# A language tower on one Trainium2 core: the first group's output projection, norm and turn are placed earlier in the banded attention loop

## The chip, the cores and the metric

The kernel is one program on one core of a Trainium2 chip. The metric is device time in microseconds (us) of one execution. Before the change three runs gave 1850.09, 1851.66 and 1854.64 us, with the median 1851.66 us. The engines are named as in the profile: PE is the matrix engine (PEld its weight loads), DVE the vector engine, ACT the scalar engine, POOL the GpSimd engine, SP the queue that issues the DMAs.

## The reference, cut to what matters

2048 tokens (8 sequences of 256) with 192 features pass four layers of banded attention with 12 heads of 16 features and a hidden layer of 768. After them come a cross-covariance attention, an expert layer with 4 experts, a full attention and an expert layer with 8 experts, which the change does not touch.

```python
h = layer_norm(emb_word[input_ids] + emb_pos[:S][None], emb_ln_s, emb_ln_b)
for l in range(L):                                     # L = 4
    q, k, v = heads(h @ Wq[l] + bq[l]), heads(h @ Wk[l] + bk[l]), heads(h @ Wv[l] + bv[l])
    a = band_attention(q, k, v, mask)                  # each query sees keys within 64 positions
    a = a.transpose(0, 2, 1, 3).reshape(B, S, Hd)
    h = layer_norm(h + a @ Wo[l] + bo[l], ln1_s[l], ln1_b[l])
    f = jax.nn.gelu(h @ W1[l] + b1[l], approximate=False)
    h = layer_norm(h + f @ W2[l] + b2[l], ln2_s[l], ln2_b[l])
```

## The kernel before, in words

Every engine has its own program, written out in order, and waits for the others on counting semaphores. The order in which work stands is therefore fixed by the code. The tokens lie in 16 tiles of 128 (`NT`), in 4 groups (`NG`) of 4 tiles (`GT`). A tile of `h` or of the attention's result `xn` must have its features on the partitions before a projection can read it. So it is turned: PE transposes it in two halves (line 417), ACT copies it into `xx` (line 638), DVE takes what the rounding left (lines 751 and 752). `xn` is turned for the output projection (kind 1 in `turned`, called "att" in the loop), `h` for the hidden layer (kind 2).

The attention loop of a layer (`pe_attention`, `act_attention`, `dve_attention`) has 96 iterations p, each for one head of one sequence. PE computes scores (lines 528 and 530), DVE their negated maximum (778), ACT the exponentials (671), PE turns the probabilities (549), ACT and DVE split them in a high part (684) and a low part (785), and PE multiplies with the values (570 to 572). After every sixth iteration DVE sums and inverts the denominators (803, 808 and 811, here the "finish"), and POOL scales the result into `xn` (1028). The loop of DVE goes on after its last maximum, until the last values are finished; this is called the drain below.

At even iterations a side step stands in the loop. `STEPS` places the projections of later groups ("chunk", "v") and the turns of `h` that feed them ("tile"). `LATE` places, in iterations 70 to 92, four turns of `xn` (tiles 0 to 3), four output projections of these tiles ("out", PE lines 445 to 449 and DVE line 741, which adds the residual into `h`), and four more turns of `xn` (tiles 4 to 7). All of these side steps share one PSUM bank, so a step waits until the one before it has been read. DVE takes statistics of group 0 at iteration 88 (884 and 888), POOL computes the inverse deviation (972 and 973), and DVE normalises the four tiles in iterations 94 to 101 (`dve_norm_step`: line 834 at even steps, 840 and 843 at odd ones).

After the loop PE projects the output of tiles 4 to 7 (`pe_out_group`; DVE adds at 875), turns `h` of group 0 (`pe_turn(pe, it, 2, 0, 8)`), and then begins the hidden layer. `pe_hidden` has steps n = 0 to 25: a step computes one block of 128 hidden features for a group of 512 tokens (five matmuls, lines 435 to 439, a "hidden block" below), ACT applies the Gelu (720), and two steps later PE multiplies with the second weight (631, 16 matmuls). `under` places turns and output projections of later groups between these steps: group 1 of `h` before step 2, group 2 of `xn` before step 3, the output of group 2 before step 5, and so on. `dve_tail` and `pool_tail` follow this order; the norm after the loop is lines 918 to 927. The first projections of the next layer stand between the last hidden blocks.

Of the kernel before, what the change touches and what calls it, by code (L numbers as in the profile page):

```python
# [34 lines left out]
NG, GT = 4, 4  # L35
# [19 lines left out]
LATE = (70, 72, 74, 76, 78, 80, 82, 84, 86, 88, 90, 92)  # L55
TURNED = ((1, 0), (1, 1), (2, 0), (2, 1), (1, 2), (2, 2), (1, 3), (2, 3))
# [49 lines left out]
def build_tower(nc, a, out, stop=None):  # L106
    ctx = ExitStack()
    with ctx:
# [256 lines left out]
        def step(p, banded):  # L365

            g, k = p // PAIRS_G + 1, p % PAIRS_G
            if banded and p in LATE:
                i = LATE.index(p)
                return ("att", "out")[i // GT % 2], i % GT + GT * (i // (2 * GT)), None  # L370
            if g < NG and k in STEPS:
                kind, i = STEPS[k]
                if kind != "tile":
                    return kind, g, i
                if g + 1 < NG:
                    return kind, GT * (g + 1) + i, None
            return None

        def pe_step(pe, it, p, banded, w, w_out, tile, xx):
# [4 lines left out]
            if back:  # L384
                kind, a, b = back[-1]
                if kind == "chunk":
                    pe.wait_ge(qf_ready.sem, qf_ready.at(it, 3 * a + b + 1))
                elif kind == "v":
                    pe.wait_ge(vf_ready.sem, vf_ready.at(it, 4 * a + b + 1))
                elif kind == "tile":  # L390
                    pe.wait_ge(xx_ready.sem, xx_ready.at(*xx(a + 1)))
                elif kind == "att":
                    pe.wait_ge(xx_ready.sem, xx_ready.at(it, turned(1, a) + 1))
                else:
                    pe.wait_ge(o_read.sem, o_read.at(it, a + 1))
# [5 lines left out]
            elif kind == "tile":  # L401
                tile(a, True)
            elif kind == "att":
                pe_transpose(pe, it, turned(1, a), a, xn, att_ready, it, a // 2 * 2 + 2, True)
            else:
                if a % GT == 0:
                    pe.wait_ge(wb_ready.sem, wb_ready.at(it, 1))
                    pe.wait_ge(xx_ready.sem, xx_ready.at(it, turned(1, a + GT - 1) + 1))
                pe_tokens(bank[BM[0]][:, 0:D], w_out, 0, D, a).then_inc(o_done.sem, 1)
# [94 lines left out]
        def under(turn, out=None, first=None):  # L504

            steps = {}
            for g in range(NG - 1):
                steps[FC * g + 2] = lambda g=g: turn(2, g + 1)
                if g + 2 < NG:
                    steps[FC * g + 3] = lambda g=g: turn(1, g + 2)  # L510
# [94 lines left out]
        def pe_out_group(pe, it, w, g):  # L605

            for t in range(GT * g, GT * g + GT):
                pe.wait_ge(xx_ready.sem, xx_ready.at(it, turned(1, t) + (3 if t % GT < 2 else 1)))
# [4 lines left out]
        def pe_hidden(pe, it, w, w2, sigs, before):  # L613

            u_done, f_ready, y_done, y_read = sigs
            for n in range(NG * FC + 2):
# [8 lines left out]
                if n >= 2:  # L625
                    g, c = (n - 2) // FC, (n - 2) % FC
                    pe.wait_ge(f_ready.sem, f_ready.at(it, n - 1))
                    for t in range(GT):
# [64 lines left out]
        def act_attention(act, it, banded, tile):  # L693

            for p in range(PAIRS + 3):
# [6 lines left out]
                if step(p, banded):  # L702
# [5 lines left out]
                    elif kind == "att":  # L708
                        act_split(act, it, turned(1, a), a, True)

# [17 lines left out]
        def dve_step(dve, ch, it, p, banded, tile):  # L728

            if p and step(p - 1, banded):  # L730
# [5 lines left out]
                elif kind == "att":  # L736
                    dve_split(dve, it, turned(1, a), a, True)
                elif kind == "out":
# [4 lines left out]
            if banded and p == LATE[2 * GT - 1] + 4:  # L743
                dve_stats(dve, ch, it, 0, 0, o_read)
            if banded:
                dve_norm_step(dve, ch, it, p - LATE[2 * GT - 1] - 10, NORMED.index((1, 0)) + 1, 0, 0)

# [183 lines left out]
        def dve_tail(dve, ch, it, opening):  # L931
# [9 lines left out]
            dve_turn(dve, it, 2, 0)  # L941
            for g in range(NG + 1):
# [8 lines left out]
                if g + 2 < NG:  # L951
# [759 lines left out]
        def _(pool):  # L1711
# [27 lines left out]
            def pool_layer(it, opening):  # L1739
# [21 lines left out]
                for f in range(NT - 5, NT):  # L1761
                    if f == NT - 3:
# [62 lines left out]
        def _(act):  # L1825
# [6 lines left out]
            def act_layer(it, opening):  # L1832
                act_attention(act, it, True, first_split(it))
                act_turn(act, it, 2, 0)
# [186 lines left out]
        def _(pe):  # L2021
# [14 lines left out]
            def pe_layer(it, opening):  # L2036
                pe_attention(pe, it, True, wa, first_turn(it), lambda n: (it, n), wb)
                pe_out_group(pe, it, wb, 1)
                pe_turn(pe, it, 2, 0, 8)
                pe_hidden(pe, it, wb, w2[0], tok_hidden,  # L2040
                          under(lambda k, g: pe_turn(pe, it, k, g, 12 if (k, g) == (2, 2) else
                                                     16 if (k, g) == (2, 3) else None),
# [181 lines left out]
```

## Time and profile before

| | us |
|---|---|
| median of the three runs | 1851.66 |
| the profiled execution's own time | 1853.58 |
| its span, first to last instruction | 1851.5 |
| PE busy in the span | 1469.3 (79%) |
| DVE busy | 1243.0 (67%) |
| ACT busy | 979.6 (53%) |
| POOL busy | 818.5 (44%) |

The profiled execution took 1853.58 us, 2.1 us more than its span, and lies inside the range of the three runs. Its mean granted PE clock is 0.899. A busy share is a mean over stages with different limits: in the attention loop DVE is nearly always busy, in the hidden layer PE is. The rows of the windows below are of layer 0, the last of the first group of layer 3. In a row of the timeline the number in brackets is how long the engine was idle before that row, and what ended the idleness. A row's start minus the start of the row before is what the instruction costs in a busy queue, since the ends overlap with the next start.

### The profile page before, as it was taken

What the parts mean: (1) busy time and instruction counts of PE and PEld (TensorE: products, weight loads), DVE (VectorE), ACT (ScalarE), POOL (GpSimd) and SP (SyncE); (2) the same over time, 40 slices, a digit from 0 to 9 for tenths busy, and PEclk for the clock granted to TensorE, in tenths of its full rate; (3) what the DMA queues carried; (4) which work ended last, traced back from release to release, by engine and by line L of the source; (5) the groups of instructions that cost most, each with busy time, mean ns of one, the idle gap of its engine ahead of it and who ended that gap; (6) DMA issues with size and microseconds to landing.
All of it is one profiled execution on the core that took longest, in us unless ns stands there. A gap on an engine that the chain in (4) does not pass through costs nothing.

```text
span 1851.5 us, 39522 instructions
## 1 busy us (share of the span) xinstructions
PE 1469.3 (79%) x13098; PEld 1230.7 (66%) x13098; DVE 1243.0 (67%) x3542; ACT 979.6 (53%) x2391; POOL 818.5 (44%) x1177
## 2 busy tenths in 40 slices
PE   0589889888898987998879769759658887599991
PEld 0467678677686776777767648539646666489991
DVE  4788966889668887768886642434388897434444
ACT  0478633788335885358863123235348882155550
POOL 5577233774236852357623410125456421145540
PEclk9999999999899998999989857679869996589996
DMA  4666101743007440054600000147534411268765
GB/s 120 172 152 124 31 1 39 164 96 77 1 5 177 99 93 1 1 133 96 143 3 1 9 6 1 35 147 237 163 87 104 106 35 35 80 203 244 236 208 178
DMA packets 144278, 177.87 MB, mean 96 GB/s; under 512 B 22096, under 2 KB 106128, under 8 KB 143952
## 3 DMA queue, kind: packets, MB, share of 16 engines
q1 hardware_dynamic: 136784, 158.18, 33.5%
q0 software_dynamic: 7296, 17.18, 2.8%
q8 instruction: 108, 1.77, 0.4%
q14 instruction: 90, 0.74, 0.1%
HBM read 132.96 MB, written 42.34 MB: 95 GB/s over the span
## 4 chain that ended last, share of the span: by engine, by line
PE 53%; DVE 26%; issue 9%; POOL 4%; DMA 4%; ACT 2%; SPq 2%; DVEq 0%; POOLq 0%; ACTq 0%
DVE ptl L785 7%; PE bank L1459 7%; PE bank L631 7%; PE bank L549 3%; DVE neg_max L778 3%; PE bank L417 2%; PE bank L570 2%; PE bank L435 2%; PE bank L437 2%; PE bank L436 2%; PE bank L1445 2%; PE bank L438 2%; PE bank L439 2%; PE bank L530 2%; DVE xx L752 2%
## 5 line engine op out<-in xcount | busy, mean ns | idle before, releaser
L671 ACT ACTIVATE prob<-bank,neg_max 128x192 f32<-128x192 f32 (+1 forms) x960 | 407.3, 437 | 115.8 <-DVE neg_max L778 102.1
L778 DVE TENSOR_REDUCE neg_max<-bank 128x2 f32<-128x384 f32 (+1 forms) x480 | 274.4, 573 | 85.9 <-PE bank L530 85.0
L785 DVE TENSOR_TENSOR ptl<-bank,pth 128x384 f16<-128x384 f32 (+1 forms) x480 | 276.1, 575 | 4.9 <-ACT pth L684 4.1
L549 PE MATMUL bank<-ident,prob 128*128 128x128 f32 x1536 | 268.5, 288 | 0.0
L684 ACT ACTIVATE pth<-bank 128x384 f16<-128x384 f32 (+1 forms) x480 | 244.5, 509 | 9.1 <-PE bank L549 8.9
L638 ACT ACTIVATE xx<-bank 128x256 fp32r<-128x256 f32 x256 | 95.6, 386 | 196.4 <-PE bank L417 192.4
L530 PE MATMUL bank<-kx,qx 96*128 96x192 bf16 (+1 forms) x960 | 166.3, 255 | 1.1 <-DVE xx L752 1.1
L549 PEld LDWEIGHTS bank<-ident,prob 128*128 128x128 f32 x1536 | 163.0, 143 | 0.0
L570 PE MATMUL bank<-v,pth 128*128 128x33 bf16 x1152 | 138.3, 180 | 20.7 <-DVE ptl L785 17.8
L720 ACT ACTIVATE fbuf<-bank,b 128x512 f32<-128x512 f32 x96 | 65.9, 687 | 155.3 <-PE bank L439 155.3
L631 PE MATMUL bank<-w,fbuf 128*128 128x192 f32 x768 | 140.7, 327 | 2.0 <-DVE h L875 2.0
L972 POOL TENSOR_SCALAR rstd<-mv 128x4 f32<-128x4 f32 x52 | 13.3, 255 | 287.1 <-DVE mv L888 280.9
L631 PEld LDWEIGHTS bank<-w,fbuf 128*128 128x128 f32 x768 | 128.5, 190 | 12.2 <-issue 5.2
L572 PE MATMUL bank<-v,ptl 128*128 128x33 bf16 x1152 | 136.4, 178 | 0.0
L571 PE MATMUL bank<-v,pth 128*128 128x16 bf16 x1152 | 132.6, 170 | 0.0
L528 PE MATMUL bank<-mask,ident 128*128 128x384 bf16 x384 | 128.5, 335 | 2.7 <-DVE xx L752 1.1
L1382 POOL DMA_INDIRECT y_rows<-vf,mask x68 | 78.9, 1160 | 117.0 <-DVE vf L1536 101.3
L570 PEld LDWEIGHTS bank<-v,pth 128*128 128x128 f16 x1152 | 99.4, 96 | 42.8 <-DVE ptl L785 42.2
L530 PEld LDWEIGHTS bank<-kx,qx 96*128 96x128 bf16 x960 | 94.3, 100 | 34.6 <-issue 3.1
L417 PE MATMUL bank<-ident,h 128*128 128x128 f32 x256 | 52.4, 310 | 81.4 <-DVE h L927 46.4
L1459 PE MATMUL bank<-w,fbuf 128*128 128x192 f32 x552 | 112.1, 327 | 0.0
L417 PE MATMUL bank<-ident,xn 128*128 128x128 f32 x256 | 57.0, 338 | 66.1 <-DVE xn L898 32.4
(295 smaller groups left out, 4519.2 us busy)
## 6 DMA issues: line engine op xcount, KB each, us to landing
xn<-in_e_seg SPq DMA_DIRECT2D x34, 768.0 KB, 6.6
w<-in_e_w SPq DMA_DIRECT2D x23, 576.0 KB, 4.1
qk_rows<-fbuf SPq DMA_DIRECT2D x128, 96.0 KB, 2.3
qx<-qk_rows SPq DMA_DIRECT2D x35, 288.0 KB, 4.0
kx<-qk_rows SPq DMA_DIRECT2D x35, 288.0 KB, 5.8
qk_rows<-w SPq DMA_DIRECT2D x80, 96.0 KB, 2.3
qx<-qk_rows SPq DMA_DIRECT2D x35, 192.0 KB, 4.6
kx<-qk_rows SPq DMA_DIRECT2D x35, 192.0 KB, 5.4
```

The source lines that it names most:

```text
L417: last = nc.tensor.transpose(o[:, c * P:c * P + P], src[:, t, c * P:c * P + P], ident[:, :])
L530: last = nc.tensor.matmul(o[:, qt, :], qx[0:ROWS, b % 3, hd, qt * P:qt * P + P], kx[0:ROWS, b % 3, hd, keys(qt, banded)], start=not banded ...
L549: last = nc.tensor.transpose(bank[BT[p % 2]][:, c * P:c * P + P], probs_at(p, banded, c * P, P), ident[:, :])
L570: nc.tensor.matmul(o, pth[:, p % 3, w], v[sums], start=first, stop=False)
L571: nc.tensor.matmul(o[third], pth[:, p % 3, w], v[lows], start=False, stop=False)
L572: return nc.tensor.matmul(o, ptl[:, p % 2, w], v[sums], start=False, stop=stop)
L631: last = nc.tensor.matmul(bank[BY[t]][:, 0:D], fbuf[:, (n - 2) % 4, t * P:t * P + P], w2[:, c, :], start=(c == 0), stop=(c == FC - 1))
L671: nc.scalar.activation(probs_at(p, banded, qt * n, n), scores_at(p, n)[:, qt, :], ACT.Exp, bias=neg_max[:, b % 2, hd, qt:qt + 1], scale=1. ...
L684: nc.scalar.activation(pth[:, p % 3, 0:n], bank[BT[p % 2]][:, 0:n], ACT.Copy).then_inc(hi_ready.sem, 1)
L778: nc.vector.tensor_reduce(neg_max[:, b % 2, hd, :], scores_at(p, D if banded else S), AX.X, ALU.max, negate=True).then_inc(max_ready.sem, 1)
L785: nc.vector.tensor_tensor(ptl[:, p % 2, 0:n], bank[BT[p % 2]][:, 0:n], pth[:, p % 3, 0:n], ALU.subtract)\
L1459: last = nc.tensor.matmul(bank[BY[2 * (G % 2) + s]][:, 0:D], fbuf[:, n % 4, s * P:s * P + P], w2_e[G % 3][:, c, :], start=(c == 0), stop=( ...
```

## The change: what it does

The side steps in the loop are laid out anew. The four turns of `xn` of group 0 move from iterations 70 to 76 to 52, 54, 58 and 60, where the last group of queries has no "tile" steps. The four output projections move from 78 to 84 to 70 to 76, the turns of `xn` of tiles 4 to 7 from 86 to 92 to 78 to 84. The statistics of group 0 move from iteration 88 to 80, its norm steps from 94 to 101 to 86 to 93. The turn of the normed `h` of group 0, which stood after the loop, becomes four side steps of kind "h" at iterations 88 to 94, on PE, ACT and DVE. POOL computes the inverse deviation one scaling step earlier. Nothing is computed anew and nothing is left out.

After the loop the hidden layer now follows the output projections of tiles 4 to 7 directly. The turn of group 2 of `xn` moves from step 3 to step 1 of the hidden layer, that of group 1 of `h` from step 2 to step 4. At step 2 PE gets one more wait, for the last finish, since the second product writes banks that the attention has used.

```diff
--- before.py
+++ after.py
@@ -54,4 +54,6 @@
          14: ("v", 0), 16: ("v", 1), 18: ("v", 2), 20: ("v", 3)}
-LATE = (70, 72, 74, 76, 78, 80, 82, 84, 86, 88, 90, 92)
-TURNED = ((1, 0), (1, 1), (2, 0), (2, 1), (1, 2), (2, 2), (1, 3), (2, 3))
+LATE = {52: ("att", 0), 54: ("att", 1), 58: ("att", 2), 60: ("att", 3), 70: ("out", 0), 72: ("out", 1), 74: ("out", 2), 76: ("out", 3),
+        78: ("att", 4), 80: ("att", 5), 82: ("att", 6), 84: ("att", 7), 88: ("h", 0), 90: ("h", 1), 92: ("h", 2), 94: ("h", 3)}
+LATE_STATS, LATE_NORM = 80, 86
+TURNED = ((1, 0), (1, 1), (2, 0), (1, 2), (2, 1), (2, 2), (1, 3), (2, 3))
 LAST_TURNS = ((0, 0), (0, 1), (0, 2), (1, 0), (0, 3), (1, 1), (1, 2), (1, 3))
@@ -368,4 +370,3 @@
             if banded and p in LATE:
-                i = LATE.index(p)
-                return ("att", "out")[i // GT % 2], i % GT + GT * (i // (2 * GT)), None
+                return LATE[p] + (None,)
             if g < NG and k in STEPS:
@@ -393,2 +394,4 @@
                     pe.wait_ge(xx_ready.sem, xx_ready.at(it, turned(1, a) + 1))
+                elif kind == "h":
+                    pe.wait_ge(xx_ready.sem, xx_ready.at(it, turned(2, a) + 1))
                 else:
@@ -404,2 +407,4 @@
                 pe_transpose(pe, it, turned(1, a), a, xn, att_ready, it, a // 2 * 2 + 2, True)
+            elif kind == "h":
+                pe_transpose(pe, it, turned(2, a), a, h, h_ready, it, normed(1, a), True)
             else:
@@ -507,5 +512,5 @@
             for g in range(NG - 1):
-                steps[FC * g + 2] = lambda g=g: turn(2, g + 1)
+                steps[FC * g + (2 if g else 4)] = lambda g=g: turn(2, g + 1)
                 if g + 2 < NG:
-                    steps[FC * g + 3] = lambda g=g: turn(1, g + 2)
+                    steps[FC * g + (3 if g else 1)] = lambda g=g: turn(1, g + 2)
                     if out:
@@ -607,3 +612,7 @@
             for t in range(GT * g, GT * g + GT):
-                pe.wait_ge(xx_ready.sem, xx_ready.at(it, turned(1, t) + (3 if t % GT < 2 else 1)))
+                pe.wait_ge(xx_ready.sem, xx_ready.at(it, turned(1, t) + 1))
+                if g == 2 and t % GT < 2:
+                    pe.wait_ge(xx_ready.sem, xx_ready.at(it, turned(2, t - 2) + 1))
+                elif g == 3 and t % GT < 2:
+                    pe.wait_ge(xx_ready.sem, xx_ready.at(it, turned(1, t + 2) + 1))
                 if t % GT >= 2:
@@ -627,2 +636,4 @@
                     pe.wait_ge(f_ready.sem, f_ready.at(it, n - 1))
+                    if n == 2:
+                        pe.wait_ge(sums_ready.sem, sums_ready.at(it, NT))
                     for t in range(GT):
@@ -709,2 +720,4 @@
                         act_split(act, it, turned(1, a), a, True)
+                    elif kind == "h":
+                        act_split(act, it, turned(2, a), a, True)
 
@@ -737,2 +750,4 @@
                     dve_split(dve, it, turned(1, a), a, True)
+                elif kind == "h":
+                    dve_split(dve, it, turned(2, a), a, True)
                 elif kind == "out":
@@ -742,6 +757,6 @@
                         .then_inc(o_read.sem, 1)
-            if banded and p == LATE[2 * GT - 1] + 4:
+            if banded and p == LATE_STATS:
                 dve_stats(dve, ch, it, 0, 0, o_read)
             if banded:
-                dve_norm_step(dve, ch, it, p - LATE[2 * GT - 1] - 10, NORMED.index((1, 0)) + 1, 0, 0)
+                dve_norm_step(dve, ch, it, p - LATE_NORM, NORMED.index((1, 0)) + 1, 0, 0)
 
@@ -940,3 +955,3 @@
             out(1)
-            dve_turn(dve, it, 2, 0)
+            dve_turn(dve, it, 1, 2)
             for g in range(NG + 1):
@@ -950,3 +965,3 @@
                     dve_stats(dve, ch, it, 1, g - 1, y_read)
-                if g + 2 < NG:
+                if g and g + 2 < NG:
                     dve_turn(dve, it, 1, g + 2)
@@ -1761,3 +1776,3 @@
                 for f in range(NT - 5, NT):
-                    if f == NT - 3:
+                    if f == NT - 4:
                         pool_rstd(pool, ch, it, NORMED.index((1, 0)) + 1, 0, 1e-12)
@@ -1833,3 +1848,2 @@
                 act_attention(act, it, True, first_split(it))
-                act_turn(act, it, 2, 0)
                 act_hidden(act, it, b1[0], tok_hidden, ACT.Gelu,
@@ -2038,6 +2052,4 @@
                 pe_out_group(pe, it, wb, 1)
-                pe_turn(pe, it, 2, 0, 8)
                 pe_hidden(pe, it, wb, w2[0], tok_hidden,
-                          under(lambda k, g: pe_turn(pe, it, k, g, 12 if (k, g) == (2, 2) else
-                                                     16 if (k, g) == (2, 3) else None),
+                          under(lambda k, g: pe_turn(pe, it, k, g, {(1, 2): 8, (2, 2): 12, (2, 3): 16}.get((k, g))),
                                 lambda g: pe_out_group(pe, it, wb, g),
```

PE after the loop, layer 0, before the change. The first row is the last matmul of the output projection of tile 7; 435 to 439 are one hidden block each, 417 with `h` a turn of one group.

```order
L449 MATMUL bank<-wb_second_lo,xx 128x192
L417 MATMUL bank<-ident,h 128x128 x8
L435 MATMUL bank<-xx,wb_hi 128x512
...
L439 MATMUL bank<-xx,wb_second_lo 128x512
L417 MATMUL bank<-ident,h 128x128 x8
L435 MATMUL bank<-xx,wb_hi 128x512
...
L631 MATMUL bank<-w_0,fbuf 128x192 x4
L417 MATMUL bank<-ident,xn 128x128 x8
```

The same place after the change (the lines are those of the new file: 454 for 449, 422 for 417, 440 to 444 for 435 to 439, 642 for 631).

```order
L454 MATMUL bank<-wb_second_lo,xx 128x192
L440 MATMUL bank<-xx,wb_hi 128x512
...
L444 MATMUL bank<-xx,wb_second_lo 128x512
L422 MATMUL bank<-ident,xn 128x128 x8
L440 MATMUL bank<-xx,wb_hi 128x512
...
L642 MATMUL bank<-w_0,fbuf 128x192 x4
L422 MATMUL bank<-ident,h 128x128 x8
```

One turn, that of group 0 of `h`, is gone from here, and the first turn between the hidden blocks is that of `xn`. 

DVE in the drain, layer 0, before: from the low part of iteration 92 (785) to the residual of tiles 4 to 7 (875).

```order
L785 TENSOR_TENSOR ptl<-bank,pth 128x384
L840 SCALAR_TENSOR_TENSOR h<-hb,rstd,ln_b 128x128
L843 SCALAR_TENSOR_TENSOR h<-hb,rstd,ln_b 128x128
L785 TENSOR_TENSOR ptl<-bank,pth 128x384
L834 SCALAR_TENSOR_TENSOR hb<-h,mv,ln_s 128x192
...
L803 SCALAR_TENSOR_TENSOR rs<-stats,pad_keys,bank 128x6 x2
L808 TENSOR_REDUCE au<-bank 128x192
L811 RECIPROCAL rs<-rs 128x12
L875 TENSOR_TENSOR h<-bank,hb 128x192 x4
```

The same place after the change (800 for 785, 818 to 826 for 803 to 811, 890 for 875).

```order
L800 TENSOR_TENSOR ptl<-bank,pth 128x384
L826 RECIPROCAL rs<-rs 128x12
L800 TENSOR_TENSOR ptl<-bank,pth 128x384 x3
L818 SCALAR_TENSOR_TENSOR rs<-stats,pad_keys,bank 128x6 x2
L823 TENSOR_REDUCE au<-bank 128x192
L826 RECIPROCAL rs<-rs 128x12
L890 TENSOR_TENSOR h<-bank,hb 128x192 x4
```

The norm steps have left the drain. They now stand inside the loop; this is DVE of layer 0 after the change, from iteration 88 (849 and 855, 858 are the norm steps, 793 the maximum, 766 and 767 the split of a turned tile).

```order
L849 SCALAR_TENSOR_TENSOR hb<-h,mv,ln_s 128x192
L793 TENSOR_REDUCE neg_max<-bank 128x2
L800 TENSOR_TENSOR ptl<-bank,pth 128x384
L766 TENSOR_TENSOR xx<-bank,xx 128x128
L767 SCALAR_TENSOR_TENSOR xx<-xx,columns,bank 128x128
L855 SCALAR_TENSOR_TENSOR h<-hb,rstd,ln_b 128x128
L858 SCALAR_TENSOR_TENSOR h<-hb,rstd,ln_b 128x128
L818 SCALAR_TENSOR_TENSOR rs<-stats,pad_keys,bank 128x6 x2
L823 TENSOR_REDUCE au<-bank 128x192
```

## Rows read from the trace of the kernel before

**Rows 1.** Windows view: stretch, length, PE PEld DVE ACT POOL busy, clock, DMA; loop.

```profile
159.26:172.72 13.46, 11.73 (x160) 9.05 (x161) 11.42 (x30) 12.13 (x35) 9.20 (x13) 1.00 0.27 63
...
183.96:195.45 11.49, 10.35 (x145) 8.24 (x143) 11.27 (x33) 10.43 (x32) 6.40 (x13) 1.00 0.62 138
195.45:206.15 10.70, 9.63 (x131) 7.89 (x130) 9.60 (x27) 8.40 (x24) 4.27 (x6) 1.00 0.01 2
206.15:218.08 11.93, 9.70 (x138) 7.54 (x136) 11.73 (x37) 9.82 (x30) 2.16 (x4) 1.00 0.01 2
...
942.42:955.61 13.19, 10.97 (x138) 8.75 (x136) 11.77 (x37) 10.24 (x31) 2.16 (x4) 0.87 0.01 2
```

**Rows 2.** Windows view, loop's end to hidden step 5: layers 0, 1, all four.

```profile
225.21:250.63 25.42, 19.48 (x101) 15.67 (x96) 15.62 (x56) 8.99 (x18) 7.15 (x12) 0.80 0.00 1
469.87:495.68 25.81, 21.11 (x100) 17.10 (x96) 15.73 (x56) 8.99 (x18) 7.15 (x12) 0.74 0.00 1
...
sum 103.20, PE 82.39 PEld 66.33 DVE 62.77 ACT 35.96 POOL 28.57; mean PE 20.60 PEld 16.58 DVE 15.69 ACT 8.99 POOL 7.14
```

**Rows 3.** Windows view, the rest of the hidden layer, layer 0.

```profile
250.63:322.58 71.95, 67.01 (x380) 58.88 (x379) 49.09 (x173) 24.88 (x46) 26.89 (x41) 1.00 0.10 24
```

**Rows 4.** PE's timeline after the loop, layer 0: start, duration, engine, line.

```profile
225.21 0.34 PE L445 MATMUL bank<-wb_hi,xx 128*128 128x192 f32 x1
...
227.75 0.50 PE L445 MATMUL bank<-wb_hi,xx 128*128 128x192 f32 x1 [1.20 <-DVE h L875]
...
229.97 1.41 PE L417 MATMUL bank<-ident,h 128*128 128x128 f32 x4
...
234.76 0.80 PE L435 MATMUL bank<-xx,wb_hi 128*128 128x512 f32 x1 [1.06 <-DVE xx L752]
...
238.47 0.60 PE L417 MATMUL bank<-ident,h 128*128 128x128 f32 x4
...
241.05 0.48 PE L435 MATMUL bank<-xx,wb_hi 128*128 128x512 f32 x1
...
242.30 1.46 PE L631 MATMUL bank<-w,fbuf 128*128 128x192 f32 x8
243.60 0.60 PE L417 MATMUL bank<-ident,xn 128*128 128x128 f32 x4
...
245.74 0.48 PE L435 MATMUL bank<-xx,wb_hi 128*128 128x512 f32 x1
```

**Rows 5.** Windows view, the stretch of low clock at the loop's end, layer 1.

```profile
466.29:483.35 17.06, 13.98 (x80) 10.98 (x79) 13.78 (x47) 4.48 (x8) 6.40 (x11) 0.50 0.00 0
```

**Rows 6.** DVE's timeline, end of the loop and drain, layer 0.

```profile
209.69 1.13 DVE L884 BATCH_NORM_STATS2 stats<-h 128x6 f32<-128x192 f32 x4
...
211.07 0.53 DVE L778 TENSOR_REDUCE neg_max<-bank 128x2 f32<-128x384 f32 x1
...
217.62 0.29 DVE L751 TENSOR_TENSOR xx<-bank,xx 128x128 fp32r<-128x128 f32 x1
...
218.08 0.55 DVE L778 TENSOR_REDUCE neg_max<-bank 128x2 f32<-128x384 f32 x1
...
219.01 0.41 DVE L834 SCALAR_TENSOR_TENSOR hb<-h,mv,ln_s 128x192 f32<-128x192 f32 x1
219.34 0.56 DVE L778 TENSOR_REDUCE neg_max<-bank 128x2 f32<-128x384 f32 x1
...
220.27 0.35 DVE L840 SCALAR_TENSOR_TENSOR h<-hb,rstd,ln_b 128x128 f32<-128x128 f32 x1
...
220.79 0.35 DVE L803 SCALAR_TENSOR_TENSOR rs<-stats,pad_keys,bank 128x6 f32<-128x6 f32 x2
...
222.45 0.50 DVE L785 TENSOR_TENSOR ptl<-bank,pth 128x384 f16<-128x384 f32 x1
...
224.34 0.56 DVE L785 TENSOR_TENSOR ptl<-bank,pth 128x384 f16<-128x384 f32 x1
...
227.32 0.56 DVE L875 TENSOR_TENSOR h<-bank,hb 128x192 f32<-128x192 f32 x2
```

## The prediction

> **What bounds the kernel now.** I read the windows view of a layer first, then the timelines of PE and DVE where it showed a change of limit. In the loop DVE sets the pace: in iterations 70 to 78 of layer 0 it is busy 11.27 of 11.49 us, in 86 to 94 11.73 of 11.93 us, while PE has 10.35 and 9.70 us of work [rows 1]. The reader is to see that a window of eight iterations is as long as DVE's work in it plus about 0.2 us. The exception is a window with side steps heavy for PE: with four output projections (78 to 86) DVE works 9.60 of 10.70 us. In the hidden layer PE sets the pace, 67.01 of 71.95 us at full clock [rows 3], so what is won or lost before it shifts all that follows. Between the two lies the stretch from the first output projection after the loop (I call its start O, 225.21 in layer 0) to that of group 2. It takes 25.42 us in layer 0 and 103.20 us over the four layers, 25.80 each, of which PE is busy 20.60, at a mean granted clock of 0.80 in layer 0 [rows 2].
>
> PE's timeline shows what that stretch holds [rows 4]. PE waits 1.20 us for DVE's residual, then turns `h` of group 0: from 229.97 to 234.76, 4.79 us, for eight transposes that wait for ACT's copies and DVE's splits in turns. Everything from 227.75 to nearly 238.47 stands in a stretch at the lower of the clock's two levels, 1.2 instead of 2.4 GHz: a pair of output projections takes 2.22 us there (227.75 to 229.97) against 1.34 (225.21 to 226.55) before. In layer 1 the low clock spans 17.06 us and begins at 466.29, before O at 469.87 [rows 2, 5].
>
> **The change part by part: the loop.** The prices come from DVE's starts [rows 6]. An iteration without a side step costs 0.93 us (218.08 to 219.01), a split 0.46 (217.62 to 218.08), an even norm step 0.33 (219.01 to 219.34), an odd one 0.52 (220.27 to 220.79), the statistics 1.38 (209.69 to 211.07).
>
> Iterations 52 to 62 get four splits, 1.84 us of DVE, four ACT copies and eight transposes. DVE is idle there 13.46 - 11.42 = 2.04 us [rows 1], so the bounds are 0 and 1.84. Much of the idleness is one wait at the projection in iteration 56, where no split stands, and ACT has only 1.33 us left for its four copies. I take 1.4.
>
> Iterations 70 to 78 get the projections for the turns. That is the window 78 to 86 of before, 10.70 us, with most of a second finish in it, which I put at 0.4: 11.1 against 11.49, so -0.4 (bounds -0.8 and 0).
>
> Iterations 78 to 86 get four splits and the statistics, which is what 86 to 94 held: 11.93 against 10.70, +1.2.
>
> Iterations 86 to 94 lose one split and the statistics and get eight norm steps: 4 x (0.33 + 0.52) - 0.46 - 1.38 = +1.56. Iteration 94 loses a norm step, -0.33.
>
> The drain, from the last maximum (219.34) to O, took 5.87 us. Of DVE's norm steps 2.22 us leave it ahead of the last low part, and one split (0.46) comes in, so the bounds are -1.76 and 0. But the low part of one iteration lets PE turn the one two later, and ACT and DVE follow: 222.45 to 224.34 is 1.89 us for two iterations, DVE's own work in it barely more. With the norm steps gone this chain is late next, and I take -0.4.
>
> Sum of the loop: 1.4 - 0.4 + 1.2 + 1.56 - 0.33 - 0.4 = +3.0 us a layer. The new turns wait on PE for the norm of the tile, one iteration earlier on DVE. Behind them in PE's queue stand the next scores; DVE needs these only after its next maximum, so I price the wait at nothing, and if that cover is gone it costs up to 0.3 a step, 1.2 a layer. POOL's inverse deviation comes before a scaling that is not due yet. SP issues nothing new and is moved past nothing.
>
> **The stretch after O.** The finish starts with the last values, as the norm steps that stood before it are gone; PE's 1.20 us of waiting shrink to 0.3 (bounds 0 and 1.20). Then, at full clock: a pair of projections 1.25, the wait 0.3, the second pair 1.25, hidden block 0 1.25 (241.05 to 242.30), the turn of `xn` in step 1 at 2.58 (the price of 238.47 to 241.05, the same kind with a Gelu ahead of it), block 1 1.25, block 2 with its product 2.55 (241.05 to 243.60), the same for step 3, the turn of `h` in step 4 at 2.14 (243.60 to 245.74), and step 4 2.55 [rows 4]. Sum: 17.7 us. The turn in step 4 needs the norm of group 1, whose path over POOL starts with DVE's statistics as before, and it is due some 13 us after O; that norm lies under steps 1 to 3.
>
> The low clock is the unknown. It costs nothing if PE stays at full clock, and if it stays low for ten us of work 5. In layer 0 two blocks took 3.71 us (234.76 to 238.47) against 2.5 at full clock, so some 2.4 us of low clock came after the blocks had begun [rows 4]; now they begin within 3 to 5 us of O. I take five us of low clock, 2.5 lost: 20.2 us against 25.80, -5.6 a layer, bounds -8.1 and -3.1.
>
> One more term: PE has fewer matmuls per us in iterations 86 to 94, about 9.5 in 13.5 us against 9.70 in 11.93, and layer 3 shows what a low stretch costs there, 13.19 us at clock 0.87 against 11.93 at 1.00 [rows 1]. I take a third of it, +0.4.
>
> The page "TensorE: Matmul & The Clock Gate" of the Trainium skill (section "What's actually happening") says that the lower clock is the default state and that activity releases it. By it the gap-free blocks after O shorten the low stretch, but the thinner stretch before O may call it earlier. Which of the two is larger the rule does not tell; the rows price both, and the first would give rival B, the second rival D.
>
> **Sum.** +3.0 + 0.4 - 5.6 = -2.2 us a layer, -8.8 in four. The profiled execution took 1853.58 us, so 1844.8; it lies 1.9 above the median of the runs, and from the median, 1851.66, it is 1843.
>
> **The rivals.** B, the clock stays high: with PE busy from O on, no low stretch or a very short one. -8.1 + 3.0 = -5.1 a layer, 1831. For it speaks the missing gap of 4.79 us, against it that in layer 1 the low clock came 3.6 us before O.
>
> C, the stall is moved, not removed: the turn of `xn` in step 1 has no product beside it, and DVE comes to it only after four residuals and the statistics, ACT only after the first Gelu. If it costs what the turn after the loop did, 4.79 instead of 2.58, the layer gains nothing: 1852. Against it speaks that the statistics (1.38) fit under block 0.
>
> D, slower: the low clock begins with the norm steps. The place is iteration 86 to O, about 19 us. The price from layer 3: 1.26 us for 13 percent of 13.19, which at half rate is 3.4 us of low clock, so 0.37 us for each. Nineteen cost 7.0, the layer +4.4, the kernel 1869. It decides from 2.6 / 0.37 = 7 us of low clock before O in each layer. For it speaks that layer 3 dropped there once; against it that layer 0, with the same load, kept the full clock in its loop's end [rows 1].
>
> **How the numbers follow.** The forecast has 0.54, with its own range 1838 to 1848; B 0.18, C 0.17, D 0.11. A difference under 0.3%, 5.6 us, cannot be told from no change here. Faster by more: 0.48 of the forecast's and B, 0.66. Within: C and 0.05 of the forecast's, 0.22. Slower: D and the rest, 0.12. The range reaches to B and C and leaves most of D out: 1830 to 1854.
>
> **What would show it.** The window of iterations 86 to 94 should be 13.3 to 13.5 us, 78 to 86 11.9, 52 to 62 14.8, and the drain about 5.5. From O to the output of group 2 it should be 19 to 22 us, with block 0 right behind the fourth projection and the turn of `xn` at 2.6. The forecast is wrong if that stretch is over 23 us or the loop longer by over 4.5. The rest of the hidden layer should stay at about 72.

## The result and the profile after

The changed kernel took 1841.12 us (median of nine runs, 1835.38 to 1846.83), the kernel before beside it 1854.93 (nine runs, 1850.09 to 1862.84). The ratio is 0.9919, with a 95% interval of 0.9898 to 0.994. The forecast was 1843, a gain of 8.8 us; the gain between these medians is 13.8. Two later sets of six runs gave 0.993 (0.9914 to 0.9946) and 0.9916 (0.9886 to 0.9947).

The page of the profiled execution, which with 1835.38 us was the fastest of the nine, shows nearly the same work in a shorter span:

```profile
span 1833.3 us, 39538 instructions
PE 1455.2 (79%) x13098; PEld 1223.2 (67%) x13098; DVE 1242.2 (68%) x3542; ACT 979.3 (53%) x2391; POOL 815.4 (44%) x1177
```

The windows view answers to [rows 1] with the first four rows (iterations 52 to 62, 70 to 78, 78 to 86, 86 to 94 of layer 0), and then 86 to 94 of layer 1:

```profile
159.08:174.15 15.07, 12.81 (x173) 10.30 (x174) 13.22 (x38) 13.11 (x39) 9.45 (x13) 1.00 0.28 66
...
185.16:197.16 12.00, 11.20 (x155) 9.56 (x154) 10.33 (x28) 9.70 (x28) 6.46 (x13) 1.00 0.49 117
197.16:208.96 11.80, 9.07 (x127) 6.87 (x124) 11.76 (x39) 9.37 (x28) 5.48 (x8) 1.00 0.01 2
208.96:221.97 13.01, 10.29 (x130) 7.22 (x128) 13.01 (x39) 10.16 (x30) 0.89 (x2) 1.00 0.00 1
451.06:464.35 13.29, 11.16 (x130) 8.36 (x128) 13.11 (x39) 10.39 (x30) 0.88 (x2) 0.87 0.01 1
```

DVE is busy for 11.76 of 11.80 us in 78 to 86 and all the time in 86 to 94 (13.01 of 13.01). In 70 to 78 it has 1.67 us of idleness. The loop from iteration 52 to O took 69.57, 69.85, 69.49 and 69.48 us in the four layers, against 65.95, 66.59, 66.85 and 67.23 before: 2.94 us more a layer. In layer 0 of the kernel before, and in layers 2 and 3 of the changed one, the low clock does not occur between iteration 52 and O, and there the difference is larger, 69.49 less 65.95 or 3.5 us: before, low clock ahead of O had lengthened layers 1 to 3 (66.59 to 67.23). The drain was 5.73 us in layer 0 and 5.65 in layers 2 and 3.

The same view of the stretch from O to the output of group 2, of layers 0 to 3 and their sum, and of the rest of the hidden layer of layer 0 (against [rows 2, 3]):

```profile
228.65:248.33 19.68, 17.37 (x92) 15.14 (x88) 12.31 (x44) 6.51 (x14) 6.89 (x12) 0.84 0.00 1
471.05:490.72 19.67, 17.36 (x92) 15.11 (x88) 12.31 (x44) 6.50 (x14) 6.87 (x12) 0.84 0.00 1
714.40:733.24 18.84, 16.25 (x93) 13.93 (x88) 12.27 (x44) 6.59 (x14) 6.87 (x12) 0.91 0.00 1
956.78:975.62 18.84, 16.24 (x92) 13.92 (x88) 12.33 (x44) 6.59 (x14) 6.88 (x12) 0.91 0.00 1
...
sum 77.03, PE 67.21 PEld 58.10 DVE 49.22 ACT 26.19 POOL 27.52; mean PE 16.80 PEld 14.53 DVE 12.30 ACT 6.55 POOL 6.88
...
248.33:320.45 72.12, 67.16 (x381) 58.98 (x380) 50.10 (x173) 25.07 (x46) 25.96 (x41) 1.00 0.10 24
```

77.03 against 103.20 is 6.54 us less a layer, and the rest did not move. So the layer gains 3.6 us from iteration 52 on, four layers 14.4; some 1.2 of it are lost again in iterations 0 to 52 and ahead of them, since at the output of group 2 of layer 3 the changed kernel is 13.2 us ahead (975.62 against 988.85). The spans differ by 18.2. The other 5.0 us lie in later stages that the change does not touch, and they are within the scatter of one program: from that point to the end the kernel before took 862.6 us, and three profiles of the changed kernel 857.7, 869.5 and 865.3 (this one, c0 and c1 below).

PE's timeline after the loop, to be read against [rows 4]:

```profile
228.65 0.51 PE L450 MATMUL bank<-wb_hi,xx 128*128 128x192 f32 x1
...
232.80 0.41 PE L454 MATMUL bank<-wb_second_lo,xx 128*128 128x192 f32 x1
233.01 0.68 PE L440 MATMUL bank<-xx,wb_hi 128*128 128x512 f32 x1
...
235.07 0.60 PE L422 MATMUL bank<-ident,xn 128*128 128x128 f32 x4
236.96 0.87 PE L422 MATMUL bank<-ident,xn 128*128 128x128 f32 x4 [1.29 <-DVE xx L767]
237.58 0.48 PE L440 MATMUL bank<-xx,wb_hi 128*128 128x512 f32 x1
...
243.77 0.60 PE L422 MATMUL bank<-ident,h 128*128 128x128 f32 x4
245.29 0.87 PE L422 MATMUL bank<-ident,h 128*128 128x128 f32 x4 [0.93 <-DVE xx L767]
245.92 0.48 PE L440 MATMUL bank<-xx,wb_hi 128*128 128x512 f32 x1
```

The hidden block at 233.01 stands right behind the last projection. The turn of `xn` takes 2.51 us (235.07 to 237.58), that of `h` 2.15 (243.77 to 245.92). In both PE waits, 1.29 and 0.93 us, for ACT's copy and DVE's split of the first tiles.

### The profile page after: what moved, and what is told of

It reads as the page before. It is cut to its first block, busy times and chain, and to the rows that moved or that the text cites. A ratio compares the mean times of both kernels' runs of the same rounds, so it can differ in the third digit from the quotient of the medians.

```text
span 1833.3 us, 39538 instructions
## 1 busy us (share of the span) xinstructions
PE 1455.2 (79%) x13098; PEld 1223.2 (67%) x13098; DVE 1242.2 (68%) x3542; ACT 979.3 (53%) x2391; POOL 815.4 (44%) x1177
## 3 DMA queue, kind: packets, MB, share of 16 engines
q8 instruction: 108, 1.77, 0.4%
## 4 chain that ended last, share of the span: by engine, by line
PE 50%; DVE 25%; issue 9%; POOL 6%; DMA 4%; ACT 3%; SPq 2%; DVEq 0%; POOLq 0%; ACTq 0%
PE bank L1474 7%; PE bank L642 7%; DVE ptl L800 7%; DVE neg_max L793 3%; PE bank L554 3%; PE bank L422 2%; PE bank L1460 2%; PE bank L440 2%; PE bank L441 2%; PE bank L442 2%; PE bank L575 2%; PE bank L443 2%; PE bank L444 2%; DVE xn L913 2%; DVE xx L767 1%
## 5 line engine op out<-in xcount | busy, mean ns | idle before, releaser
L987 POOL TENSOR_SCALAR rstd<-mv 128x4 f32<-128x4 f32 x52 | 13.2, 255 | 245.1 <-DVE mv L903 239.1
L1043 POOL TENSOR_TENSOR xn<-au,rs 128x192 f32<-128x192 f32 x80 | 41.4, 518 | 157.5 <-DVE rs L826 155.2
```

## The experiments

Each kernel is timed against the kernel before on the same chip. "The stretch" below is O to the output of group 2.

**c0_after**, the change itself, as the base of the first set.

> The changed kernel itself, as the one against which the other kernels of this call are read. By all theories it is 12 to 16 us faster than the kernel before, as its nine runs were; from the loop's end to the output of group 2 it takes 19 to 20 us a layer.

1842.49 us, 0.993 (0.9914 to 0.9946). Its stretches were 19.70, 19.82, 17.26 and 17.25 us. The windows of layers 0 and 2, and of what follows in layer 2 up to the next loop:

```profile
228.91:248.61 19.70, 17.39 (x91) 15.15 (x88) 11.28 (x44) 6.50 (x14) 7.98 (x12) 0.84 0.00 1
714.12:731.38 17.26, 14.66 (x93) 12.49 (x88) 12.73 (x44) 6.57 (x14) 7.00 (x12) 1.00 0.00 1
731.38:805.92 74.54, 69.36 (x394) 60.41 (x392) 52.61 (x185) 25.37 (x46) 27.88 (x44) 1.00 0.11 28
```

The stretch at full clock is 17.25 us, with 0.29 us of waiting between the two pairs of output projections (at 715.75); the same program paid 2.45 us more in a layer with 6.3 us of low clock (a mean clock of 0.84 over 19.70 us, the lower level being half of the full one), and 1.59 more with 3.4 us (18.84 above). The next profile, **c1_after**, had 18.84, 19.75, 19.48 and 18.84: which layers see the lower clock differs between executions.

> The changed kernel itself once more, for the two others of this call: 12 to 16 us faster than the kernel before by all theories.

1839.64 us, 0.9916 (0.9886 to 0.9947).

**e1_loop_only**: the new layout of the loop, with `h` still turned after it and the hidden order of before. The diff is against the change and shows only the two lines that matter.

```diff
-        78: ("att", 4), ..., 84: ("att", 7), 88: ("h", 0), 90: ("h", 1), 92: ("h", 2), 94: ("h", 3)}
+        78: ("att", 4), ..., 84: ("att", 7)}
 ...
                 pe_out_group(pe, it, wb, 1)
+                pe_turn(pe, it, 2, 0, 8)
```

> The kernel before with only the loop laid out anew: output projection, statistics and norm of group 0 early as in the change, but its normed tiles are still turned after the loop, and the hidden layer's order is that of before. Theory 1 (the gain comes from the turn of 4.8 us that left the stretch after the loop): iterations 52 to 95 get 2.4 us a layer longer, the drain loses 0.4, PE's wait of 1.2 us loses 0.9, so the kernel is 2 to 6 us slower than before. Rival (the gain comes from the norm that left the drain and from the clock): it keeps most of the gain, 8 to 14 us faster than before.

1853.79 us, 0.9991 (0.9977 to 1.0005): no difference that can be told, where a small loss was expected. The windows of the stretch in layers 0 and 2, and of the drain in layer 0:

```profile
227.44:251.54 24.10, 19.04 (x100) 15.07 (x96) 14.76 (x52) 8.99 (x18) 7.15 (x12) 0.86 0.00 1
717.09:740.45 23.36, 18.09 (x101) 14.50 (x96) 14.80 (x52) 8.99 (x18) 7.08 (x12) 0.93 0.00 1
222.18:227.44 5.26, 3.76 (x66) 2.73 (x67) 4.04 (x11) 3.38 (x10) 0.52 (x1) 1.00 0.02 3
```

The earlier projection and norm cost the loop 1.9 us a layer up to its last maximum. The drain (5.26 or 5.27 us in the four layers, 6.17 in the mean before) gave 0.9 back and the stretch, with its shorter low clock, 2.1 (23.7 in the mean against 25.80). So the gain does not come from the earlier projection and norm by themselves.

**e2_old_hidden_order**: the change, but with the turns between the hidden blocks as before (`h` of group 1 before step 2, `xn` of group 2 before step 3).

```diff
-                steps[FC * g + (2 if g else 4)] = lambda g=g: turn(2, g + 1)
+                steps[FC * g + 2] = lambda g=g: turn(2, g + 1)
-                    steps[FC * g + (3 if g else 1)] = lambda g=g: turn(1, g + 2)
+                    steps[FC * g + 3] = lambda g=g: turn(1, g + 2)
```

> The changed kernel with the hidden layer's order of before: h of group 1 is turned before step 2 and xn of group 2 before step 3. Theory 1 (the two turns had to change places, since the norm of group 1 now ends too late for step 2): PE waits 3.5 to 6 us for the norm before step 2, so the kernel is 14 to 22 us slower than the changed one, about as fast as before. Rival (the order is indifferent, the turn costs the same wherever it stands): within 4 us of the changed one.

1867.05 us, 1.0063 (1.0045 to 1.0082): 25 us slower than the change, where 14 to 22 were expected. The timeline of PE in layer 0, with DVE's last norm instruction of tile 4 (L940), and the window of the stretch in layer 2:

```profile
233.62 0.39 PE L444 MATMUL bank<-xx,wb_second_lo 128*128 128x512 f32 x1
238.09 0.34 DVE L940 SCALAR_TENSOR_TENSOR h<-hb,rstd,ln_b 128x128 f32<-128x128 f32 x1
...
238.53 0.66 PE L422 MATMUL bank<-ident,h 128*128 128x128 f32 x2 [4.51 <-issue]
...
241.60 1.11 PE L422 MATMUL bank<-ident,h 128*128 128x128 f32 x4 [1.56 <-DVE xx L765]
```

```profile
725.65:751.85 26.20, 18.88 (x93) 15.86 (x88) 13.41 (x44) 6.79 (x14) 7.17 (x12) 0.80 0.00 1
```

PE stands idle for 4.51 us ahead of the turn of group 1. The profile names no releaser, but the turn waits for the norm of that group, and DVE ends the norm of its first tile at 238.43 (L940), 0.10 us before PE goes on. With the first turn gone from here, the wait for the norm takes its place; the exchanged order is what avoids it. The low clock is longer here too (10.2 to 12.8 us a layer), so the four stretches come to 26.1 us in the mean, no shorter than before the change.

**e5_half_turns**: each turn between hidden blocks in two halves, two tiles ahead of the block and two behind it, so that the block's five matmuls run while ACT and DVE empty the shared bank. DVE's residual of a finished group stands ahead of the splits.

```diff
-            for t in range(GT * g, GT * g + GT):
+            for t in range(GT * g + 2 * half, GT * g + 2 * half + 2):
 ...
                     pe_features(bank[BU[n % 2]][:, :], w, D + c * P, g).then_inc(u_done.sem, 1)
+                if n + 0.5 in before:
+                    before[n + 0.5]()
 ...
+                    if g:
+                        dve_residual(dve, ch, it, 1, g - 1)
                     dve_turn(dve, it, 2, g + 1)
```

> The changed kernel with each of the five turns between hidden blocks in two halves: two tiles before the block and two behind it, so that PE has the block to work on while ACT and DVE take the first two; DVE adds the residual of the group before ahead of the turn's splits. Theory 1 (a turn costs PE a wait for ACT and DVE, 0.9 us in the rows of before and about 2 us in step 1): 4 x 0.9 + 2.0 = 5.6 us a layer, 22 us faster than the changed kernel. Rival (DVE is late next, the wait only moves to the product behind the turn): within 6 us of the changed one.

1820.38 us, 0.9795 (0.9773 to 0.9817): 22 us faster than the change. Windows of the stretch in layers 0 and 3 and of the rest of layer 2 up to the next loop; then PE's timeline in layer 0:

```profile
230.37:245.64 15.27, 14.63 (x92) 12.27 (x88) 12.57 (x44) 6.37 (x14) 7.02 (x12) 1.00 0.00 1
939.73:957.18 17.45, 17.29 (x92) 15.00 (x88) 10.96 (x44) 6.17 (x14) 7.99 (x12) 0.82 0.00 1
718.34:791.11 72.77, 68.89 (x394) 60.26 (x393) 52.22 (x186) 25.23 (x46) 27.93 (x44) 1.00 0.12 29
```

```profile
234.36 0.60 PE L422 MATMUL bank<-ident,xn 128*128 128x128 f32 x4
234.71 0.48 PE L440 MATMUL bank<-xx,wb_hi 128*128 128x512 f32 x1
...
236.25 0.87 PE L422 MATMUL bank<-ident,xn 128*128 128x128 f32 x4
236.87 0.48 PE L440 MATMUL bank<-xx,wb_hi 128*128 128x512 f32 x1
...
258.14 0.87 PE L422 MATMUL bank<-ident,h 128*128 128x128 f32 x4 [0.68 <-DVE xx L773]
```

In the stretch the waits of 1.29 and 0.93 us are gone and a half turn costs PE 0.35 and 0.62 us; in the rest of the layer a wait stays in some of the turns, as in the last row. The stretch is 1.98 us shorter at full clock (17.25 to 15.27), the rest of layer 2 by 1.77 (74.54 to 72.77). The four stretches sum to 63.3 us against 74.0 in c0, and the rests give some 7 more: 18 us, where the two profiled executions differ by 16.7 (1843.51 and 1826.84) and the medians by 22. The 22 us that were expected priced each turn at its whole wait, 5.6 us a layer; the windows at full clock show 3.8.

**e8_half_turns_old_residual**: the same, with the residual behind the splits as in the change.

```diff
-                    if g:
-                        dve_residual(dve, ch, it, 1, g - 1)
                     dve_turn(dve, it, 2, g + 1)
```

> The kernel with the half turns, but DVE adds the residual behind the turn's splits as the changed kernel does. Theory 1 (the second half's splits then delay the residual, and PE's product of step 8 and 14 waits for it): two waits of 1.2 to 1.8 us a layer more, 8 to 14 us slower than with the residual first, 8 to 14 us faster than the changed kernel. Rival (the residual's place is indifferent): within 3 us of the kernel with the half turns.

1833.65 us, 0.9885 (0.9857 to 0.9913): 8 us faster than the change and, by the ratios, 16 slower than e5. PE's timeline in layer 0, and the window of the rest of layer 2:

```profile
264.09 1.54 PE L646 MATMUL bank<-w,fbuf 128*128 128x192 f32 x8 [1.81 <-DVE h L896]
```

```profile
731.96:807.79 75.83, 70.31 (x394) 61.74 (x393) 52.53 (x186) 24.82 (x46) 27.90 (x44) 0.98 0.12 27
```

The split into halves delays DVE's list, and the product of the next group then waits 1.81 us until the residual has freed its banks, and once more 1.82 us six steps later. The stretch at full clock is as short as in e5 (15.26 us in layers 1 and 2); all of the loss is in the rest of the layer, which also has 3.4 to 6.8 us of low clock here and none in e5. By the ratios more than half of the gain of e5 hangs on that one place in DVE's order.

**e3_filled_drain**: the change with 15 matmuls more in the drain, three at each of its iterations, into the bank of the side steps. Their results are not used.

```diff
+                if banded and p >= PAIRS:
+                    if p == PAIRS:
+                        pe.wait_ge(xx_ready.sem, xx_ready.at(it, turned(2, 3) + 1))
+                    for _ in range(3):
+                        nc.tensor.matmul(bank[BM[0]][:, 0:2 * D], ident_bf, mask[:, 0:2, :], start=True, stop=True)
```

> The changed kernel with 15 extra matmuls in each layer's drain (three in each of its five PE iterations, 384 columns, their result is read by nobody), some 2.5 us of PE work in 2 us of waiting. Theory 1 (the low clock behind the loop follows from the thin stretch ahead of it and costs 0.36 us for each us): the low stretches at the loop's end become rarer or vanish, the stretch from the loop's end to the output of group 2 falls to 17.3 us in every layer, the drain gets up to 0.5 us longer: 1 to 6 us faster than the changed kernel. Rival (the low clock does not depend on the drain): low stretches as in the changed kernel, the drain longer, 0 to 3 us slower than it.

1828.86 us, 0.9853 (0.9832 to 0.9873). The windows of the stretch and of the drain in layer 0:

```profile
229.95:247.02 17.07, 14.71 (x88) 12.55 (x86) 12.77 (x44) 6.23 (x14) 7.01 (x12) 1.00 0.00 1
223.58:229.95 6.37, 5.65 (x81) 4.01 (x82) 4.48 (x14) 4.64 (x11) 0.52 (x1) 1.00 0.01 3
```

No stretch of this profile has a low clock (17.06 or 17.07 us in all four layers); the drain is some 0.7 us longer, the stretch 2.2 shorter than the mean of the change's profile, so 6 us in four layers. By the medians and by the ratios e3 is 11 to 14 us faster than the change. The mean granted clock fits: it was 0.915 to 0.922 in the five runs of e3 and 0.900 to 0.913 in all 21 runs of the change.

One profile does not prove the cause, though, for the profile of e9 below, where nothing is filled, has no low clock in its four stretches either. Over all kernels with the order of the change, with whole or half turns, none of the 8 stretches behind a filled drain (e3, e11) has a low clock, and 12 of 28 behind an unfilled one have none. Nor is there a further gain behind the layers: from the last maximum of the fourth loop to the full attention e3 took 404.3 us, the change 412.7, 416.0 and 410.8, but e10 took 404.6 without filling and e11 412.3 with it. Why the medians differ by more than the 6 us of the layers stays open.

**e12_before_filled**: the kernel before with the same 15 matmuls.

```diff
+                    if p == PAIRS:
+                        pe.wait_ge(xx_ready.sem, xx_ready.at(it, turned(1, 7) + 1))
```

> The kernel before with the same 15 extra matmuls in each layer's drain, whose result is read by nobody. Theory 1 (the gain of the change is the turn's wait of 4.8 us that left the stretch after the loop, and only a part of it is the clock): PE still stands still during that wait, so the low clock comes back behind it; 0 to 7 us faster than before, at least 7 us slower than the changed kernel. Rival (the whole gain is the clock, which the thin drain had lowered): as fast as the changed kernel, within 3 us.

1849.68 us, 0.9971 (0.9955 to 0.9988): 5 to 6.5 us faster than before. Windows of the stretch in layers 0 and 1:

```profile
228.09:252.50 24.41, 19.05 (x95) 15.12 (x94) 15.54 (x55) 8.99 (x18) 7.09 (x12) 0.86 0.01 1
473.09:497.02 23.93, 18.07 (x96) 14.51 (x94) 15.44 (x55) 8.99 (x18) 7.10 (x12) 0.93 0.00 1
```

With 3.4 us of low clock the old order takes 23.93 us where the change, with as much, takes 18.84. That is 5.1 of the 6.54 us that the stretch gained. The clock alone is not the change's gain. In these two rows 3.4 us more of low clock cost only 0.48 us.

**e9_projections_shifted**: the change with the projections one side step later.

```diff
-... 70: ("out", 0), 72: ("out", 1), 74: ("out", 2), 76: ("out", 3), 78: ("att", 4),
+... 70: ("att", 4), 72: ("out", 0), 74: ("out", 1), 76: ("out", 2), 78: ("out", 3),
```

> The changed kernel with the four output projections in the loop at iterations 72 to 78 instead of 70 to 76; the turn of tile 4 of xn takes iteration 70. Theory 1 (a projection costs DVE 0.55 us of waiting unless a finish stands in DVE's iteration just before the one it delays, as with 72, 78 and 84): two of four are covered instead of one, iterations 70 to 86 are 0.5 to 0.6 us shorter a layer, about 2 us in all. Rival (the waiting belongs to the number of side steps, not to their place): the same length within 0.1 us.

1842.81 us, 0.9938 (0.9907 to 0.9969), not told from the change; its five runs spread from 1826.65, the profiled one, to 1851.77 us. Windows 70 to 78 and 78 to 86 of layer 0, and the stretch of layer 0:

```profile
185.16:197.00 11.84, 10.89 (x152) 9.17 (x151) 10.50 (x29) 9.83 (x29) 6.45 (x13) 1.00 0.50 119
197.00:208.54 11.54, 9.25 (x129) 7.20 (x128) 11.50 (x38) 9.09 (x27) 5.48 (x8) 1.00 0.01 2
...
228.16:245.40 17.24, 14.65 (x92) 12.48 (x88) 12.74 (x44) 6.58 (x14) 7.01 (x12) 1.00 0.00 1
```

23.38 against 23.80 us: 0.4 a layer, and the same in all four layers, short of the 0.5 to 0.6 that were expected; it is less than the runs can tell. The four stretches took 17.24 or 17.25 us, all at full clock, though the drain is that of the change. So a whole execution can keep the clock there without filling.

**e10_half_turns_shifted** is e5 with the layout of e9, **e11_all_filled** that with the 15 matmuls as well.

> Half turns and the projections at 72 to 78 together. Theory 1 (both savings add up): 2 us faster than the half turns alone, 24 us faster than the changed kernel, ratio to the kernel before 0.978 to 0.980. Rival: no more than the half turns alone.

> Half turns, projections at 72 to 78, and the filled drain together. Theory 1 (the filled drain keeps the clock high and the half turns take the waits, both add up): the stretch from the loop's end to the next loop at 93.7 to 94 us in every layer with no low clock in it, 4 to 12 us faster than the half turns alone, ratio to the kernel before 0.974 to 0.979. Rival (with half turns PE is busy enough, the filling only lengthens the drain): 0 to 3 us slower than the half turns alone.

1820.04 us, 0.9817 (0.9789 to 0.9844), and 1814.66 us, 0.9783 (0.9745 to 0.9822): neither is told from e5 by its interval, so that the savings add up is not shown. In e10's profile three of the four stretches have 6.3 to 6.8 us of low clock (17.43 to 17.56 us) and one has none (15.26); in e11's none has. The stretch of e11 in layer 0:

```profile
230.22:245.30 15.08, 14.69 (x88) 12.32 (x86) 12.58 (x44) 6.00 (x14) 7.00 (x12) 1.00 0.00 1
```

PE is busy 14.69 of 15.08 us: nothing is left to win there but work. e5, e10 and e11 all beat both kernels.

## Why the prediction was right, step by step

**What bounds the kernel.** Right. The stretch between DVE's loop and PE's hidden layer is where the time was (25.80 to 19.26 us), and the rest stayed at 72.12 against 71.95. The mechanism was right, and two of the terms below came out near their sum because errors met.

**The loop, +3.0 with +0.4 for its clock.** The loop's sum came out at +2.94 a layer, clock and all, and that it is near is luck. At full clock the loop got 3.5 us longer, not 3.0, and the clock gave 0.6 back where I had +0.4. I had put the low clock ahead of O on top of the change as if the kernel before had none; its layers 1 to 3 had it. Among the terms two erred against each other. In iterations 70 to 78 I had -0.4 and it was +0.51, outside the bounds, since I took a window of four projections with a finish from a window of before where the finishes stood elsewhere. DVE's maxima in that window, after the change:

```profile
186.74 0.56 DVE L793 TENSOR_REDUCE neg_max<-bank 128x2 f32<-128x384 f32 x1 [0.57 <-PE bank L535]
189.74 0.50 DVE L793 TENSOR_REDUCE neg_max<-bank 128x2 f32<-128x384 f32 x1
192.45 0.56 DVE L793 TENSOR_REDUCE neg_max<-bank 128x2 f32<-128x384 f32 x1 [0.54 <-PE bank L535]
195.23 0.56 DVE L793 TENSOR_REDUCE neg_max<-bank 128x2 f32<-128x384 f32 x1 [0.56 <-PE bank L535]
```

Behind a projection DVE waits about 0.55 us for the scores, unless a finish stands in the same iteration to cover it. Here one of four is covered, before two of four were. Against it, 86 to 94 cost +1.09 where I had 1.56; 0.20 us of that is idleness of DVE in the window before (11.93 less 11.73), which the norm steps filled, and the rest was not looked into. Smaller: 52 to 62 +1.61 against 1.4; 78 to 86 +1.09 (11.80) against 1.2; iteration 94 -0.31 against -0.33; and the piece between, iterations 62 to 70, which I had not priced, -0.22. In the change's profile the window 86 to 94 had low clock in one layer only, and 3.4 us of it made 13.29 us out of 13.01: 0.28 us, where the same low clock had cost 1.26 in layer 3 before.

**The drain, -0.4.** It was -0.2 at full clock (5.65 in layers 2 and 3 against 5.87 in layer 0 before) and -0.5 in the mean of the layers, where before had low clock in it. DVE's timeline shows what is late there:

```profile
225.76 0.49 DVE L800 TENSOR_TENSOR ptl<-bank,pth 128x384 f16<-128x384 f32 x1
...
227.11 1.16 DVE L800 TENSOR_TENSOR ptl<-bank,pth 128x384 f16<-128x384 f32 x2 [0.85 <-ACT pth L695]
228.85 0.35 DVE L818 SCALAR_TENSOR_TENSOR rs<-stats,pad_keys,bank 128x6 f32<-128x6 f32 x2 [0.59 <-PE bank L577]
230.12 0.36 DVE L890 TENSOR_TENSOR h<-bank,hb 128x192 f32<-128x192 f32 x1 [0.19 <-PE bank L454]
```

The chain PE, ACT, DVE of the last iterations, with waits of 0.85 and 0.59 us, is what I named as late next.

**The waits of the new turns on the norm, nothing.** Right: DVE has no idleness in 86 to 94 in layer 0.

**The stretch, 17.7 at full clock and 2.5 for the clock.** At full clock it is 17.25, with PE's wait at 0.29 as I had it (0.3) and the turns at 2.51 and 2.15 against 2.58 and 2.14. The five us of low clock that I took were 4.8 in the mean, and they cost 2.0 (19.26 less 17.25), not 2.5. The step that carried the forecast, -5.6, was too small by 0.9. Of the 6.54 us measured, 5.1 are there at a like clock (23.93 in e12 against 18.84). The other 1.4 come with the shorter low clock, 4.8 us a layer against 12.8 before. The split is rough: another pair of layers, 24.41 with 6.8 us of low clock against 19.70 with 6.3, gives 4.7, and e12's rows are of a filled drain, which made the change's own stretch 0.2 us shorter (17.06).

**The sum.** -3.6 a layer against -2.2: 0.9 of the difference is the stretch, 0.5 the loop. So the medians fell by 13.8 us and not by 8.8. That 1843 lies only 1.9 from the measured 1841.12 is luck in part: the median before, from which I counted, was 1851.66 of three runs, and with nine it is 1854.93.

**The rivals.** B, the clock stays high, is not what the profiles of the change show as a whole, but two layers of c0 had it, and all four of e9 and of e3. The profiled execution of e9 took 1826.65 us, near B's 1831. C, the stall is moved, is refuted by the turn at 2.51 us; e2 shows that it was near, since the other order of the same turns would have made the kernel slower than before. D did not come: in the change's profile no more than 4.0 us of low clock lay between iteration 86 and O, where 7 were needed. Its price does not hold in that place either: 0.37 us for each us of low clock from [rows 1], but 0.08 in iterations 86 to 94 of the change. In the stretch it is 0.39 and 0.47 by c0 and 0.14 in the old order by e12, so it belongs to the place and the order.

The page "TensorE: Matmul & The Clock Gate" of the Trainium skill, section "What's actually happening", has the lower clock as the default that activity releases. The runs agree as far as they go: with the filled drain the mean granted clock was 0.915 to 0.922 in all runs of e3, above each of the change (0.900 to 0.913). In the change itself the stretches lost low clock too (a mean granted clock of 0.84 and 0.91 against 0.80 and 0.74), which is rival B's direction. The drop in one execution and not in the next, with the same program, is not explained by anything here.

## What to carry to other kernels

A change that only takes a stall out is worth little until one has read what is late next; here the earlier norm needed both the turn in the loop and another order behind it, and either half alone gained nothing (e1) or lost (e2). Where PE turns tiles through ACT and DVE into one bank, put half of the turn on each side of an independent block, and let DVE do first what frees PE's banks: that gave more than the change itself (22 us against 14). Price a stretch at both clock levels, look whether the kernel before has the low clock in the same place, and price side steps by the waits they leave, not by the busy time of a window that resembles them. Do not read a gain of a few us in untouched stages out of one profile: the same 860 us differed by 12 us between profiles of one program.

## What the runs showed of the hardware

- The same program, executed again, had the lower clock (1.2 instead of 2.4 GHz) in other layers: the stretch was 17.25, 18.84 or 19.7 us with 0, 3.4 or 6.3 us of it.
- Untouched code behind the layers took 857.7, 865.3 and 869.5 us in three profiles of one program.
- Fifteen matmuls in each drain, whose results nobody reads, made a kernel faster by 11 to 14 us (e3, against the change) and by 5 to 6.5 us (e12, against before). In e3 they lengthened a drain by 0.7 us, and the mean granted clock was 0.915 to 0.922 in its five runs against 0.900 to 0.913 in 21 runs of the change. One profile without them (e9) had full clock in all four stretches as well.
- The price of a us of low clock was 0.39 to 0.47 us in the stretch of the change, 0.37 in iterations 86 to 94 before, 0.14 in the old order of the stretch (e12) and 0.08 in iterations 86 to 94 of the change. In none of these places was it the half that a PE at half rate would lose if it alone set the time.
